# Three convolution passes of a graph network: the dense read of the neighbour sums becomes a gather, and the own-row product moves to ScalarE

## The reference, cut to what matters

```
deg  = segment_sum(1, dst)                 # counts self-loops
dinv = rsqrt(deg)
h    = x @ W                               # 768 x 768
out  = segment_sum(h[src] * (dinv[src]*dinv[dst])[:, None], dst) + b

x2 -> x3:  x3 = layernorm(x2 + conv(x2, W, b))
x3 -> h3:  h3 = relu(conv(x3, W1, b1))
h3 -> out: out = layernorm(x3 + conv(h3, W2, b2))
```

## Time and profile before

| | us |
|---|---|
| median of 3 runs | 4126.54 |
| lowest and highest run | 4124.19, 4127.32 |
| the profiled execution | 4123.81 |
| its span, first to last instruction | 4122.1 |

### The profile page before, as it was taken

How to read it: one execution, slowest core, us unless ns; L and a number is a source line. 1 busy time by engine, 2 the same in 40 slices (tenths; PEclk the granted TensorE clock), 3 DMA queues, 4 the chain that set the end, 5 groups by cost and what they waited for, 6 DMA issues and landing times. The chain is left out here.

```text
span 4122.1 us, 64308 instructions
## 1 busy us (share of the span) xinstructions
PE 3675.4 (89%) x21456; PEld 3421.4 (83%) x21456; DVE 2531.8 (61%) x4903; ACT 1179.3 (29%) x1691; POOL 859.3 (21%) x915
## 2 busy tenths in 40 slices
PE   6999999999998883059996999997899998799999
PEld 5999999999996441039994999996799997599999
DVE  4967984277144884648883677774344443477777
ACT  2222232222222442015663222222222222222222
POOL 5620001324411003248884000003000001200000
PEclk9999999999999997579998999999999999899999
DMA  3565665445433783055665444445444444567775
GB/s 101 166 187 178 191 194 174 135 154 196 148 112 128 247 248 106 2 151 195 218 220 195 159 172 172 172 171 186 172 172 168 172 172 157 184 228 228 229 228 178
DMA packets 341341, 717.89 MB, mean 174 GB/s; under 512 B 88111, under 2 KB 141057, under 8 KB 341200
## 3 DMA queue, kind: packets, MB, share of 16 engines
q1 hardware_dynamic: 241392, 471.75, 36.2%
q10 hardware_dynamic: 67584, 154.63, 9.6%
q0 software_dynamic: 32224, 89.68, 7.0%
HBM read 445.23 MB, written 301.21 MB: 181 GB/s over the span
## 5 line engine op out<-in xcount | busy, mean ns | idle before, releaser
L647 DVE TENSOR_TENSOR fr_lo<-fr_turned_ps,fr_hi 128x768 fp32r<-128x768 f32 x158 | 150.7, 954 | 247.0 <-ACT fr_hi L995 246.8
L2317 DVE SCALAR_TENSOR_TENSOR c3a_y<-c3a_prod,dinv,next_const 128x768 f32<-128x768 f32 x79 | 80.4, 1018 | 289.2 <-PE c3a_prod L2471 289.2
L1125 PE MATMUL fr_prod<-fr_w_hi,fr_hi 128*128 128x396 f32 x948 | 256.5, 352 | 0.0
L1125 PE MATMUL fr_prod<-fr_wu_hi,fr_hi 128*128 128x396 f32 x948 | 255.2, 350 | 0.2 <-issue 0.2
L1125 PE MATMUL fr_prod<-fr_w_lo,fr_hi 128*128 128x396 f32 x948 | 249.3, 344 | 0.0
L1125 PE MATMUL fr_prod<-fr_wu_lo,fr_hi 128*128 128x396 f32 x948 | 248.8, 343 | 0.4 <-issue 0.3
L2471 PE MATMUL cv_prod<-next_w_hi,cv_hi 128*128 128x384 f32 x948 | 248.6, 343 | 0.0
L1125 PE MATMUL fr_prod<-fr_w_hi,fr_lo 128*128 128x396 f32 x948 | 248.5, 343 | 0.0
L2471 PE MATMUL c3b_prod<-next_w_hi,c3b_hi 128*128 128x384 f32 x948 | 248.4, 343 | 0.0
L2471 PE MATMUL c3a_prod<-next_w_hi,c3a_hi 128*128 128x384 f32 x948 | 248.4, 343 | 0.0
L1125 PE MATMUL fr_prod<-fr_wu_hi,fr_lo 128*128 128x396 f32 x948 | 248.0, 343 | 0.0
(11 more groups left out here) (489 smaller groups left out, 8842.1 us busy)
## 6 DMA issues: line engine op xcount, KB each, us to landing
fr_ins<-in_x_dram SPq DMA_DIRECT2D x156, 384.0 KB
h<-fr_outs SPq DMA_DIRECT2D x78, 396.0 KB
u<-fr_outs SPq DMA_DIRECT2D x78, 396.0 KB
up_ut<-u SPq DMA_DIRECT2D x78, 396.0 KB
agg<-fr_zrow SPq DMA_DIRECT2D x78, 390.0 KB
x<-up_x_o ACTq DMA_DIRECT2D x78, 384.0 KB
hds_row<-x SPq DMA_DIRECT2D x78, 384.0 KB
x<-hds_x_o ACTq DMA_DIRECT2D x78, 384.0 KB
```

The lines of the kernel that those rows point to most:

```text
L647: v.tensor_tensor(lo[:, s2, :, :], turned_ps[:, 0:KC, :], hi[:, s2, :, :].bitcast(F32), ALU.subtract).then_inc(split_done, 1)
L1125: made = nc.tensor.matmul(prods[s2][:, bank, 0:c1 - c0], l[:, s2, s, :], w[:, s, c0:c1], start=(s == 0 and i == 0), stop=(s == KC - 1 and ...
L2317: ec.link(dve, v.scalar_tensor_tensor(y3, p3, g["dinv"][:, bass.ds(t, 1)], c3, ALU.mult, ALU.add))
```

## The change

`dense_pass` is replaced by `conv_pass` for the three convolutions. What is computed stays the same.

- SP no longer loads `agg`. It loads `row`, and in `c3b_` also `res`.
- POOL clears a buffer `more` of four slots when the block begins; then for each tile it copies the indices, issues the tiny instruction and gathers rows of `agg` of the nodes that have incoming edges from others. From the fifth tile on it waits until `built` has freed the slot.
- ACT has a new step `scale`: x = row * own_d. Its order becomes scale(t+1), high(t), root(t-2), polish(t-3), store(t-4).
- DVE's `build` becomes x = more * has_in + x, and waits for the gather and for `scaled`. Its other steps and their order stay.
- In the pass without a residual, SP refills a row slot once ACT has scaled it (before, once DVE had built from it).
- PE's code is the same.

```diff
-        dense_pass(nc, g, "cv2", "conv", a, x3, row=x2, agg=agg, res=x2)
+        conv_pass(nc, g, "cv", x2, agg, x3, res=x2)
...
-        dense_pass(nc, g, "c3a", "conv", a, h3, row=x3, agg=agg)
+        conv_pass(nc, g, "c3a", x3, agg, h3)
...
-        dense_pass(nc, g, "c3b", "conv", a, out, row=h3, agg=agg, res=x3)
+        conv_pass(nc, g, "c3b", h3, agg, out, res=x3)
...
         @block.sync
...
-                for name, table, w in loads:
-                    sp.dma_start(ins[name][0:n, slot, :], tile_rows(table, t)[:, 0:w]).then_inc(loaded[slot], 16)
+                sp.dma_start(rows_in[0:n, slot, :], tile_rows(row, t)).then_inc(loaded[slot], 16)
+                if apart:
+                    sp.dma_start(res_in[0:n, slot, :], tile_rows(res, t)).then_inc(loaded[slot], 16)
...
         @block.gpsimd
+            nc.gpsimd.memset(more[:, :, :], 0.0).then_inc(cleared, 1)
+            pool.wait_ge(cleared, 1)
+
+            def fetch(t, slot, turn):
+                if at_least(t, UNROLL):
+                    pool.wait_ge(built, t - UNROLL + 1)
+                nc.gpsimd.tensor_copy(ix[:, slot:slot + 1], g["in_i"][:, bass.ds(t, 1)]).then_inc(indexed, 1)
+                pool.wait_ge(indexed, t + 1)
+                take_wait(nc, g, scrap_p[:, 0:1])
+                nc.gpsimd.indirect_dma_start(more[:, slot, :], None, agg, bass.IndirectOffsetOnAxis(ap=ix[:, slot:slot + 1], axis=0),
+                                             bounds_check=N - 1, oob_is_err=False).then_inc(more_in[slot], 16)
...
         @block.vector
...
-                    v.scalar_tensor_tensor(x[:, s2, :], r, g["own_d"][:, bass.ds(t, 1)], ag, ALU.mult, ALU.add).then_inc(built, 1)
+                dve.wait_ge(more_in[slot], turn * 16 + 16)
+                dve.wait_ge(scaled, t + 1)
+                v.scalar_tensor_tensor(x[:, s2, :], more[:, slot, :], g["has_in"][:, bass.ds(t, 1)], x[:, s2, :],
+                                       ALU.mult, ALU.add).then_inc(built, 1)
...
         @block.scalar
+            def scale(t, slot, turn):
+                act.wait_ge(loaded[slot], turn * (16 * L) + 16 * L)
                 if at_least(t, 2):
                     act.wait_ge(turned, t - 1)
+                nc.scalar.activation(x[:, slot % 2, :], rows_in[:, slot, :], ACT.Copy, scale=g["own_d"][:, bass.ds(t, 1)]).then_inc(scaled, 1)
```

More of the change, by code:

```diff
@@ L1993, in _, with conv_pass @@
             over_tiles(pe, step, 1)
[L1996 to L2024, removed]
+def conv_pass(nc, g, tag, row, agg, out, res=None):
     with ExitStack() as ctx:
@@ L2030, in dense_pass @@
         sem = semaphores(nc, ctx, f"{tag}_")
[L2032 to L2040, removed]
+        norm, apart = res is not None, res is not None and res is not row
@@ L2041, in dense_pass @@
+        L = 2 if apart else 1
+        rows_in = sb("row", [P, UNROLL, D])
+        res_in = sb("res", [P, UNROLL, D]) if apart else rows_in
+        more = sb("more", [P, UNROLL, D])
+        ix = sb("ix", [P, UNROLL], I32)
+        x, y = sb("x", [P, 2, D]), sb("y", [P, 2, D])
+        hi, lo = sb("hi", [P, 2, KC, P], F32R), sb("lo", [P, 2, KC, P], F32R)
+        outs = sb("outs", [P, UNROLL, D])
+        scrap, scrap_p = sb("scrap", [P, 1]), sb("scrap_p", [P, 1])
         stats, mv = sb("stats", [P, 2, 2, 6]), sb("mv", [P, 2, 2])
@@ L2087, in dense_pass @@
[L2087 to L2099, removed]
@@ L2101, in all_stored @@
-        def all_stored(eng):
-            for j in range(UNROLL):
-                eng.wait_ge(stored[j], 16 * n_store * ((NT - 1 - j) // UNROLL + 1))
+        cleared, indexed, scaled, built = sem("cleared"), sem("indexed"), sem("scaled"), sem("built")
+        turned, hi_done, split_done = sem("turned"), sem("hi_done"), sem("split_done")
+        multiplied, prod_read, summed = sem("multiplied"), sem("prod_read"), sem("summed")
+        halved, spread, rooted, shifted, polished = sem("halved"), sem("spread"), sem("rooted"), sem("shifted"), sem("polished")
@@ L2105, in _ @@
+        block = ctx.enter_context(nc.Block())
         @block.sync
         def _(sp):
[L2107 to L2139, removed]
+            def step(t, slot, turn):
+                if not live(t):
+                    return
@@ L2443, in turn_over @@
                 if at_least(t, 1):
-                    pe.wait_ge(split_done if split else hi_done, t)
-                s2 = slot % 2
-                for s in range(S):
-                    if kind == "update":
-                        src = ins["res"][:, slot, s * P:(s + 1) * P] if s < KC else x[:, s2, (s - KC) * P:(s - KC + 1) * P]
-                    elif kind == "heads":
-                        src = x[:, s2, s * P:(s + 1) * P] if s < KC else ins["row"][:, slot, (s - KC) * P:(s - KC + 1) * P]
-                    else:
-                        src = x[:, s2, s * P:(s + 1) * P]
-                    last = nc.tensor.transpose(turned_ps[:, s, :], src, g["ident"][:, :])
@@ L2454, in turn_over @@
-                last.then_inc(turned, 1)
+                    pe.wait_ge(split_done, t)
+                for s in range(KC):
+                    made = nc.tensor.transpose(turned_ps[:, s, :], x[:, slot % 2, s * P:(s + 1) * P], g["ident"][:, :])
+                made.then_inc(turned, 1)
             def multiply(t, slot, turn):
                 s2 = slot % 2
-                pe.wait_ge(split_done if split else hi_done, t + 1)
+                pe.wait_ge(split_done, t + 1)
                 if at_least(t, 2):
@@ L2473, in multiply @@
-                last.then_inc(multiplied, 1)
+                for s in range(KC):
+                    for i, (l, w) in enumerate(((hi, w_hi), (hi, w_lo), (lo, w_hi))):
+                        for a in range(2):
+                            made = nc.tensor.matmul(prods[s2][:, a, 0:HALF], l[:, s2, s, :], w[:, s, a * HALF:(a + 1) * HALF],
+                                                    start=(s == 0 and i == 0), stop=(s == KC - 1 and i == 2))
+                made.then_inc(multiplied, 1)
             def step(t, slot, turn):
```

321 lines of the change are left out of this document (57 added, 264 removed).

## The result

The changed kernel takes 4130.82 us (median of 20 runs, 4124.65 to 4140.29) against 4122.86 us for the kernel before (20 runs beside them): the ratio is 1.0021, with a 95% interval of 1.0014 to 1.0028, so 5.8 to 11.5 us slower, 8.7 at the middle (the two medians differ by 7.96). The sum had +9.0. The profiled execution took 4133.67 us with a span of 4131.8.

The account below looks back on a forecast made before the run. The prediction took PE's own work, 6.91 us a tile, to bound the loops. Only the starts would cost: 3.6 + 3.5 + 1.9 = +9.0 us, giving 4132.8 profiled, 4135.5 us against the runs' median; range 4130 to 4142 us.

Parts of the forecast that it names:

- Removed loads, VectorE's build, ScalarE's scale, POOL's fetch in the loop, all at nothing: In the three convolution loops, these four parts would cost or save nothing, being covered by PE's 6.91 us a tile.
- Clear and issue, 3.79 us: At each pass's start, from POOL's start of clearing `more` to the issue of the first gather: 3.79 us.
- Landing in `cv_`: First gather in `cv_`, from issue to use: 3.9 us, making the first build +3.6 us later.
- lower bound of 3.15: Least landing time of a gather at a pass's start: 3.90 us seen for 128 whole rows, less 300 KB not moved.
- Landing in `c3a_`: First gather in `c3a_`, from issue to use: again 3.9 us, making the first build +3.5 us later.
- Landing in `c3b_`: First gather in `c3b_`, landing among eight loads: 5.5 us from issue to use, making the first build +1.9 us later.
- a sign of being wrong: At the starts of the passes, a gather's landing under 3 or over 6 us would show the prediction wrong.
- PE's half-speed stretch, at zero: At pass starts, PE's granted clock of 0.50 moves along with the start; a microsecond either way, taken at zero.
- The loops keep 6.91 us a tile: In the changed profile, the convolution loops would keep 6.91 us a tile with PE busy throughout.
- Faster: In the loops, reads of `agg` slow tiles unseen; shortening tiles by 2% would give 4103 us; chance 0.03.
- Crowded start: In `c3a_` and `c3b_` the first gather queues behind row loads, landing in 7.92 us: +15.4, 4142 us; chance 0.11.
- Stalled loop: Gather or ScalarE's scale comes late each tile; half a microsecond a tile gives +118 us, 4254 us; chance 0.04.

Follow-up runs that it names:

- e1_dense_first: Changed kernel, but the first four tiles of each pass read `agg` by plain SP loads, with no clearing; ratio 0.9999 to the kernel before.
- e7: Changed kernel with ScalarE's multiplication only: `agg` comes by plain SP loads for every tile and POOL's block is gone; ratio 0.9997 to the kernel before.
- e8: Changed kernel with POOL's clearing and gathers only: VectorE multiplies in its build, without ScalarE's scale or the factor has_in; ratio 1.0009 to the kernel before.
- e0_again: The changed kernel run once more, unaltered, beside the kernel before; ratio 1.0013.
- e3_hold: Changed kernel, clearing kept, but SP issues the loads of tile 1 onwards only after the first gather has landed; ratio 1.0021 to the kernel before.
- e4_no_clear_hold2: Changed kernel without clearing, gathering into edge-stage buffers, SP holding loads from tile 2 on until the first gather has landed; ratio 0.9995 to the kernel before.
- e6_ahead: Changed kernel without clearing; first four tiles' rows and the first gather are requested during the edge stage; 4109.93 us, ratio 0.9977 to the kernel before.
- e9_frame: Changed kernel's rewritten function with both parts undone: plain SP loads of `agg`, VectorE multiplying in its build; ratio 0.9989 to the kernel before.
- e2: Changed kernel, but gathering into edge-stage buffers that already hold finite numbers, so nothing is cleared; ratio 1.0000 to the kernel before.
- e13_ahead_busy: As e6_ahead, plus unread matmuls for TensorE: 20 at the end of the edge stage, 6 at the pass's start; ratio 0.9978 to the kernel before.

## Why the prediction was right

Right: slower, by +8.7 us against the +9.0 of the sum, inside the range, and by the mechanism given. That it came out so close is luck: the starts cost 2.4 us more than the sum had, and the loops, which it had unchanged, gave 3.8 back. The time itself, 4130.82 us, lies 4.7 under the 4135.5 forecast and only 0.8 above the lower end of the range, mostly because the kernel before has 4122.86 in 20 runs where the forecast started from 4126.54 in three. And +0.21% stands on the bound of 0.2% between the two outcomes to which the prediction gave 0.50 and 0.47, so it favours neither.

- *Removed loads, VectorE's build, ScalarE's scale, POOL's fetch in the loop, all at nothing:* right. e1_dense_first keeps nearly all of them and costs nothing, and e7 and e8 split them without a trace in PE's time. The scale took 0.93 us, where I estimated 1.03. In `c3b_` it makes some `high` start late, as I had said it might, by up to 0.3 us (0.6 in e0_again), and the tile keeps its 6.900 us.
- *Clear and issue, 3.79 us:* right to the hundredth (3.79, 3.78, 3.77).
- *Landing in `cv_`, 3.9 us:* it took 3.51, so +3.2 for +3.6. The clean value, without loads around it, is 2.8 us (e3_hold), below my lower bound of 3.15: the part that isn't movement is shorter than the row of 3.90 let one think.
- *Landing in `c3a_`, 3.9 us:* the step that was most wrong. It took 5.72 (+5.3 for +3.5). I wrote that "then two more" loads follow as soon as ScalarE has scaled, and then priced the pass as if they did not matter. e8, where the refills wait for the build, lands in the 3.90 I had taken (one profile).
- *Landing in `c3b_`, 5.5 us:* it took 6.59, 6.49 in the second profile (+2.9 for +1.9). That is over the 6 us which the prediction had set as a sign of being wrong: the loads ahead delay the gather more than I allowed for (3.01 in e3_hold, which holds six of the eight back).
- *PE's half-speed stretch, at zero:* right in the sum. From the second transposes to the granted clock's return to 1.00 it takes 5.5, 5.0 and 5.3 us before, 6.1, 3.8 and 6.1 after, and in another execution of the same changed kernel 3.5, 3.0 and 6.1. It varies by over 2 us from one execution to the next.
- *"The loops keep 6.91 us a tile":* it was 6.917 and became 6.900, which makes 3.8 us over the 228 tiles read. The rival *Faster* asked whether a tile could shorten and looked only for a cause in the traffic. The tile did shorten, by 0.24%, for a cause that no term of mine looked at: the diff gives the pass other buffers in another order.

Of the rivals, *Crowded start* came true in kind: the landings of `c3a_` and `c3b_` at 5.7 and 6.6 lie about halfway from 3.9 to its 7.92. *Stalled loop* and *Faster* (by traffic) are refuted. The gather's landing, 2.8 us on quiet DMA engines (e3_hold), is nearer to the 2.2 us that I estimated in the prediction from the Trainium skill, DMA: Bandwidth & Descriptors, section Anatomy of one DMA — SWDGE (gpsimd) path, than to my 3.9; beside loads (up to 6.7 us) the trace does not agree with it. By the terms of the sum, 2.2 us in all three passes would have taken 6.7 us off it, not about 6.

## What to carry to other kernels

A transfer that is off the critical path in the loop can be the whole cost of a pass at its start: price the first tile by itself, with every load that its queues issue before and just behind it, also those that a buffer freed earlier now lets go. Two remedies worked here: to issue the gather without a clearing and with fewer loads around it (e4_no_clear_hold2 brings the starts back to the 32 us of before), and to ask for the first tile's data in the stage before (e6_ahead goes on to 19.5, and pays 6.4 of it in that stage). Each added hold must be followed to the next tile, or it only moves the wait (e3_hold). When a function is rewritten, its buffers move too; to judge a change of some tenths of a per cent, run the new function with the change undone (e9_frame) and keep the places of the buffers.

## What the hardware showed unexpectedly

- The places of buffers in SBUF alone (16 bytes ahead of them and the order of two) change the time of a loop that TensorE bounds: 525.66 or 524.40 us for 76 tiles, the same to 0.02 us in every pass of every kernel with the one layout or the other.
- A gather of about 87 KB lands 2.8 to 3.0 us behind its issue on quiet DMA engines, 3.2 to 3.5 where four row loads of 384 KB were issued some 2 to 4 us earlier (`cv_`), and 5.6 to 6.7 where four to eight were issued about it (e2, `c3b_` of e4) or eight ahead of it (`c3b_`). In `c3a_`, where two more were issued 0.1 to 1.9 us behind it, it took 5.25 to 6.30 us, against 3.90 in the one profile without them.
- At the start of `cv_` the granted clock rose to 1.00 at 2269.1 us, 4.5 us into the pass, when TensorE had been given matmuls during its wait (e13_ahead_busy), and was at 0.50 until 2274.1, 10.7 us into it, without them (e6_ahead). In e13_ahead_busy it then fell once more for 3.4 us, and the kernel was no faster.
